# A fused block on one core: expert rows summed in memory by accumulating scatters, and the expert pairs spread over two more units

## What is computed

```python
probs = softmax(x @ Wr); topw, topi = top_k(probs, 4)      # 2048 tokens, 32 experts
shared = silu(x @ Wsg) * (x @ Wsu) @ Wsd                     # 512 -> 1408 -> 512
shared = shared * sigmoid(x @ Wse)
pos = position of each (token, k) in its expert's queue      # kept where pos < 64
ye = (silu(xe @ Wg) * (xe @ Wu)) @ Wd                        # per expert: 64 slots, 512 -> 352 -> 512
out = shared.at[tok].add(ye[sel, posc] * (w * valid))        # up to 4 rows of ye for each token
return x + gb * out
```

## Time and profile before

| | us |
|---|---|
| median of 3 runs | 750.3 (747.75 to 751.67) |
| the profiled run | 753.79 |
| its span, first to last instruction | 751.6 |
| TensorE busy in it | 685.0 |
| VectorE busy | 401.0 |
| ScalarE busy | 296.5 |
| GpSimd busy | 223.0 |

### The profile page before, as it was taken

How to read it: one execution, slowest core, us unless ns; L and a number is a source line. 1 busy time by engine, 2 the same in 40 slices (tenths; PEclk the granted TensorE clock), 3 DMA queues, 4 the chain that set the end, 5 groups by cost and what they waited for, 6 DMA issues and landing times.

```text
span 751.6 us, 9183 instructions
## 1 busy us (share of the span) xinstructions
PE 685.0 (91%) x3297; PEld 476.0 (63%) x3297; DVE 401.0 (53%) x735; ACT 296.5 (39%) x565; POOL 223.0 (30%) x217
## 2 busy tenths in 40 slices
PE   4798888999998799999999999999998999998894
PEld 3565656777666567886665655565564566686673
DVE  3758759678588857762224222122122133688897
ACT  3434785665746623323225333133232143323311
POOL 1254464745436200001000001001000002788883
PEclk9789998999999999999999999999999999999998
DMA  8750000000131004007777877767988772666664
GB/s 270 258 197 0 1 15 28 15 29 15 42 134 63 14 1 140 1 1 258 269 284 291 321 277 263 272 248 284 310 303 302 267 267 80 181 173 193 210 189 147
DMA packets 48328, 124.27 MB, mean 165 GB/s; under 512 B 6152, under 2 KB 10268, under 8 KB 48284
## 3 DMA queue, kind: packets, MB, share of 16 engines
q1 hardware_dynamic: 41884, 102.72, 38.4%
q0 software_dynamic: 6400, 20.98, 9.9%
HBM read 110.83 MB, written 12.85 MB: 165 GB/s over the span
## 4 chain that ended last, share of the span: by engine, by line
PE 37%; DVE 10%; DMA 9%; issue 7%; ACT 3%; POOL 2%; SPq 1%; DVEq 0%; POOLq 0%; ACTq 0%
PE bank L1663 14%; PE bank L1718 9%; PE bank L1675 7%; PE bank L1735 5%; DMA expert_rows<-ye 4%; DMA egu<-in_L_ffn_Wu_dram 3%; DVE egu L1361 2%; ACT xsH L851 1%; DVE prod L1207 1%; DMA xg<-h_rows,slot_tok 1%; DVE ed L1361 1%; DVE egu L1362 1%; PE bank L1706 1%; PE bank L1766 1%; ACT prodH L865 1%
## 5 line engine op out<-in xcount | busy, mean ns | idle before, releaser
L1663 PE MATMUL bank<-xsH,wguH 128*128 128x512 f32 x352 | 144.1, 409 | 7.4 <-issue 2.9
L1663 PE MATMUL bank<-xsL,wguH 128*128 128x512 f32 x352 | 138.3, 393 | 0.0
L1663 PE MATMUL bank<-xsH,wguL 128*128 128x512 f32 x352 | 138.0, 392 | 0.0
L668 POOL DMA_INDIRECT xg<-h_rows,slot_tok x16 | 15.4, 962 | 334.6 <-PE bank L1706 242.1
L1718 PE MATMUL bank<-egu,xeT 128*64 128x352 f32 x512 | 82.6, 477 | 8.9 <-DMA egu<-in_L_ffn_Wu_dram 8.8
L1663 PEld LDWEIGHTS bank<-xsH,wguH 128*128 128x128 f32 x352 | 66.7, 189 | 33.7 <-issue 15.1
L1675 PE MATMUL bank<-wdH,prodH 128*128 128x512 f32 x176 | 74.2, 421 | 12.1 <-DVE prodL L1209 9.6
L865 ACT ACTIVATE prodH<-prod 128x512 fp32r<-128x512 f32 x38 | 24.0, 631 | 140.3 <-DVE prod L1207 133.9
L1663 PEld LDWEIGHTS bank<-xsL,wguH 128*128 128x128 f32 x352 | 66.4, 189 | 14.7
L1663 PEld LDWEIGHTS bank<-xsH,wguL 128*128 128x128 f32 x352 | 66.6, 189 | 12.9 <-issue 0.7
L1207 DVE TENSOR_TENSOR prod<-bank,silu 128x512 f32<-128x512 f32 x38 | 26.2, 688 | 83.3 <-PE bank L1663 60.2
(11 more groups left out here) (225 smaller groups left out, 1117.5 us busy)
## 6 DMA issues: line engine op xcount, KB each, us to landing
egu<-in_L_ffn_Wg_dram SPq DMA_DIRECT2D x32, 704.0 KB
egu<-in_L_ffn_Wu_dram SPq DMA_DIRECT2D x32, 704.0 KB
ed<-in_L_ffn_Wd_dram SPq DMA_DIRECT2D x32, 512.0 KB, 6.1
h2T<-in_L_wmod_dram SPq DMA_DIRECT2D x6, 1024.0 KB, 9.1
ed<-in_L_ffn_Wd_dram SPq DMA_DIRECT2D x32, 192.0 KB, 7.3
expert_rows<-ye SPq DMA_DIRECT2D x17, 256.0 KB, 8.1
h_rows<-ho SPq DMA_DIRECT2D x16, 256.0 KB, 2.0
out_dram<-xres SPq DMA_DIRECT2D x16, 256.0 KB
```

What stands on the lines that cost most here:

```text
L1663: ins = mm.matmul(bk[:, :], l[f][:, w, c, :], r[:, c, :], start=(k == 0), stop=(k == 3 * C - 1))
```

## The change

Five things are changed together.

1. **Sums in memory.** `expert_rows` and the gathers from it are gone. A new array `expert_sums` has one row for each token. SP sets it to zero with 16 stores of 256 KB from the zeroed `ye`, before the first pair's weights. For each pair POOL adds the rows of `ye` to it with two scatters that accumulate in memory (one for each expert of the pair, 64 rows; the second runs over 128 rows, the first 64 of them out of bounds and so skipped). POOL waits for the first before it issues the second, since both experts may have the same token. ACT writes the next pair's rows into `ye` only when both have landed (`added`). SP no longer waits in its loop for anything that has to do with `ye`.
2. **Places.** The 49 stages are spread over the 73 places up to the end of unit 13. The pieces of the last shared weights are asked for two pairs earlier.
3. **The last part.** SP reads all sums back with five plain transfers after the last scatter. DVE joins a tile with one addition. All 16 joins and all 16 gates are on DVE, in units 14 and 15 (`JOINS`, `GATES`). In unit 15 DVE takes the four down results straight from PSUM (`scalar_tensor_tensor`), without ACT's copy.
4. **The table.** `slot_table` makes the destination table `slot_to` as well, and POOL waits for it before the first gather. `y_idx` and its four operations in `slots` are gone.
5. **Order.** `first_rows` of two tiles moves ahead of the low part of tile 1, with POOL's `first_rstd(4)`; `experts_mask` and `pairs_before` move behind the next unit's inputs; PE's `positions` moves behind the second half.

```diff
-        PLACES = [(u, k) for u in range(PAIRS_FROM[0], MERGE) for k in range(2 * PARTS[UNITS[u][0]] + GT)
+        PLACES = [(u, k) for u in range(PAIRS_FROM[0], MERGE + 2) for k in range(2 * PARTS[UNITS[u][0]] + GT)
...
+        JOINS = {(2, 2): (0, 1, 2, 3), (2, 3): (4, 5), (3, 0): (6, 7, 8), (3, 1): (9, 10, 11, 12), (3, 2): (13, 14, 15)}
+        GATES = {(2, 3): (0, 1, 2, 3), (3, 1): (4, 5), (3, 2): (6, 7, 8, 9)}
+        JOINED_FIRST = 12
...
-                    if NP // 2 + 1 <= j < NP // 2 + 4:
+                    if NP // 2 - 1 <= j < NP // 2 + 2:
...
-                    sp.wait_ge(ye_ok, j + 1)
-                    sp.dma_start(ye_dram[j * P:(j + 1) * P, :], ye[:, :]).then_inc(ye_sent, 16)
-                    sp.wait_ge(ye_sent, 16 * (j + 1))
-                    sp.sem_inc(ye_free, 1)
...
+                sp.wait_ge(added, 32 * NP)
+                for k, (i, n) in enumerate(((0, 4), (4, 4), (8, 4), (12, 3), (15, 1))):
+                    at = sums_dram[i * P:(i + n) * P, :].rearrange("(i p) h -> p i h", p=P)
...
+                def add_rows(j):
+                    pool.wait_ge(ye_ok, j + 1)
+                    for e in range(2):
+                        if j or e:
+                            pool.wait_ge(added, 16 * (2 * j + e))
+                        n = (e + 1) * CAP
+                        gp.indirect_dma_start(sums_dram[:, :], bass.IndirectOffsetOnAxis(slot_to[0:n, e, j:j + 1], axis=0),
+                                              ye[0:n, :], None, bounds_check=B * T - 1, oob_is_err=False,
+                                              compute_op=ALU.add).then_inc(added, 16)
...
                 def pair_out(j):
                     act.wait_ge(ey_full, j + 1)
-                    act.wait_ge(ye_free, j + 1)
...
+                        act.wait_ge(added, 32 * j)
...
+                    if n >= LAST_TAKEN:
+                        dve.wait_ge(d_full[m % 2], n // 2 + 1)
+                        dve.wait_ge(y_read, i + 1)
+                        v.scalar_tensor_tensor(xres[:, i, :], dB[m % 2][:, :], sigma[:, i:i + 1], xres[:, i, :],
+                                               ALU.mult, ALU.add).then_inc(d_used[m % 2], 1)
+                        return
...
+                def join(i):
+                    dve.wait_ge(y_in[i // GT if i < NT - 1 else NG], 16)
+                    p = len(PARTS) - (2 if i >= JOINED_FIRST else 1)
+                    dve.wait_ge(x_acc, tile(p, 0, i) - FIRST_TAKEN + 1)
+                    v.tensor_tensor(xres[:, i, :], xres[:, i, :], sum_at[i], ALU.add).then_inc(y_read, 1)
```

More of the change, by code:

```diff
@@ L223, in build @@
         onehot = scr[:, 512:512 + NT * TOP_K * E].rearrange("p (i k e) -> p i k e", k=TOP_K, e=E)
-        top_e, odd, pos, over, idx_f = (scr[:, at:at + NT * TOP_K].rearrange("p (i k) -> p i k", k=TOP_K)
-                                        for at in range(5120, 5120 + 5 * NT * TOP_K, NT * TOP_K))
+        top_e, odd, pos, over = (scr[:, at:at + NT * TOP_K].rearrange("p (i k) -> p i k", k=TOP_K)
+                                 for at in range(5120, 5120 + 4 * NT * TOP_K, NT * TOP_K))
         picked = scd[:, 0:NT * TOP_K * E].rearrange("p (i k e) -> p i k e", k=TOP_K, e=E)
@@ L241, in build @@
         tokB = bank[3][:, 0:3 * NP]
-        YW = TOP_K * H
-        yg = [w.rearrange("p (k h) -> p k h", k=TOP_K) for w in (scr[:, 0:YW], scr[:, YW:2 * YW], scd[:, 0:YW])]
-        NY = len(yg)
+        sum_at = ([scr[:, k * H:(k + 1) * H] for k in range(8)] + [scd[:, k * H:(k + 1) * H] for k in range(4)]
+                  + [scr[:, k * H:(k + 1) * H] for k in range(8, 11)] + [scd[:, 4 * H:5 * H]])
         MERGE = NG * (len(PARTS) - 1)
@@ L523, in _ @@
                 sp.wait_ge(zero_ok, 1)
-                sp.dma_start(ye_dram[E * CAP:E * CAP + P, :], ye[:, :]).then_inc(zero_sent, 16)
+                for i in range(NT):
+                    sp.dma_start(sums_dram[i * P:(i + 1) * P, :], ye[:, :]).then_inc(zero_sent, 16)
                 sp.wait_ge(hot_used, 2 * NG)
@@ L663, in _, with fetch_rows @@
                 gp.memset(ye[:, :], 0.0).then_inc(zero_ok, 1)
-                pool.wait_ge(tab_ok, 1)
-                for j in range(NP):
+                pool.wait_ge(tab_ok, 2)
+                def add_rows(j):
[7 more added lines that the diff above has]
+                                              compute_op=ALU.add).then_inc(added, 16)
+                def fetch_rows(j):
                     if j:
@@ L1103, in _ @@
                 first_var(4)
+                first_rows(HB + 2)
+                first_rows(HB + 3)
                 h_lo(1)
@@ L1401, in _ @@
                         first_var(5)
-                        for i in (HB + 2, HB + 3, 2, 3):
+                        for i in (2, 3):
                             first_rows(i)
@@ L1458, in _ @@
                             experts_ones()
-                        if u == EARLY and f == 1:
-                            experts_mask()
                         if f == 0 and g == 0 and p:
@@ L1501, in _ @@
                         lo_group(*UNITS[u + 1], chunks=range(C // 2, C))
-                    if u >= MERGE and not join_first(g, 2):
-                        combine(g, 2)
-                    if u >= MERGE and join_first(g, 3):
-                        for m in range(3):
-                            last_gate(g * GT + m)
-                        combine(g, 3)
+                    if u == EARLY:
+                        experts_mask()
+                        pairs_before()
+                    if not ahead:
+                        for m in range(10, NT - 1):
+                            last_gate(m)
                     down(p, g, 3)
@@ L1830, in _ @@
                         pair_stages(u, 2 * f)
-                        if u == ROUTE and f == 0:
-                            positions()
                         if u == ROUTE + 2 and f == 0:
@@ L1839, in _ @@
                         half(p, g, f, 1)
+                        if u == ROUTE and f == 0:
+                            positions()
                         pair_stages(u, 2 * f + 1)
```

136 lines of the change are left out of this document (59 added, 77 removed).

## The result

| | us |
|---|---|
| changed kernel, median of 4 runs | 726.4 (724.26 to 729.17) |
| kernel before on the same chip, median of 4 | 750.0 (747.75 to 751.67) |
| ratio | 0.969, 95% interval 0.965 to 0.973 |
| the profiled run of the changed kernel | 729.17, span 727.4 |

What follows compares the result with a forecast made beforehand. TensorE was taken as the bound, busy 685.0 of 751.6 us. The terms sum to -28.4, taking the profiled run from 753.8 to 725.4; with the median 3.5 lower, the forecast was 722 us, range 716 to 740.

Steps and rivals of the forecast that it cites:

- A: First rows of step 1: making two `xhat` rows earlier removes TensorE's idle time and a clock loss, -4.4 us.
- B: Unit 3 to unit 4: mask and scan moved behind the next inputs remove TensorE's idle time and clock loss, -3.7 us.
- C: First gather: the larger table makes POOL start later with nothing to hide it, +1.1 us, up to +2.8.
- D: Expert pairs: SP asks for weights without waiting for the `ye` store, removing TensorE's weight waits and slow clock, -11.5 us.
- E: Last part, unit 12 to the end: two units without joins, then joins and gates in units 14 and 15, -9.9 us.
- The scatters' cycle: Per pair, writing `ye` and two scatters of 7.1 us take 14.9 us, under the shortest period of 16.4: no cost.
- rival 1: Slower scatters set the pairs' pace, cycle 2 s + 0.9 for landing time s; 772 us at s = 11.2; chance 0.10.
- ScalarE never waiting: Sign in the changed profile, against scatters setting the pace: ScalarE never waits for `expert_sums` to land.
- a late scatter stops TensorE within about 2 us: Pairs: ScalarE's waits for scatters hold up `silu`, `prodH` and row copies behind them, so TensorE soon stops.
- the rival's 10 us: Scatters pacing the pairs: only short periods, 738 to 746 us, chance 0.09, or all, 772 us, chance 0.10.
- Rival 3: Gains of A and B are caught by the next engine, VectorE cancels E's; 740 us, 748 with bad D; chance 0.07.

Runs made afterwards that it cites:

- places_12: The changed kernel with the pairs' stages spread only to the end of unit 11, as in the kernel before; 737.2 us, ratio 0.982.
- before_no_wait: The kernel before, but SyncE no longer waits for the store of `ye` to land before asking for the next weights; 740.0 us, ratio 0.989.
- three_scatters: The changed kernel with a third accumulating 64-row scatter per pair, between the two, into an array nothing reads; one time of 742.2 us.

## Why the prediction was right, and where its sum was off

| term | forecast | ledger, first profiles | ledger, second profiles | timed, by the ratios |
|---|---|---|---|---|
| A | -4.4 | -0.9 | -2.9 | -3.7 |
| B | -3.7 | -2.7 | -4.0 | -3.4 |
| C | +1.1 | +2.4 | +0.2 | +3.0 |
| D | -11.5 | -13.2 | -9.6 | -8.3 |
| E | -9.9 | -9.8 | -10.6 | - |
| sum | -28.4 | -24.2 | -26.9 | |

Units 12 and 13 stand between D and E. Without pairs a unit takes 24.9 us (the first silus of units 12, 13 and 14 in places_12 are at 630.67, 655.54 and 680.45), where 24.7 was forecast. D in the ledger is first gate-up to silu, less two such units (304.4 + 14.96 - 49.8 = 269.6 in the first profile of the changed kernel against 282.75 before); E is those two units plus the last stretch (49.8 + 57.2 against 116.9). places_12, whose pairs end with unit 11, shows E by itself: 737.7 - 630.67 = 107.0, so -9.8 and -10.0 against the two profiles of before. The timed values come from undoing the step, each with 2 to 3 us either way; D's is SyncE's wait alone. Their sum with an E of -9.9 is -22.3, and -23.3 was measured by the ratio (-23.6 by the medians); with those intervals the sum alone would prove little.

**A and B** passed as argued: no `xhat` wait, the first half of unit 4 right behind unit 3, and 0.8 us in `positions` where 0.9 was forecast. In the first profile of the changed kernel they fall short, by 3.5 and 1.0 us, where the clock dips of that run lie; that run was 2.8 us above its median.

**D, mechanism right, the term mis-sized.** All its signs came: no weight wait, a mean period of 20.0, the stretch to unit 14 at 320.8 us where 320 was forecast. The after side was right. The before side was one run with 8.8 us of waits where the next had 6.9. The step that failed is the one from the profiled run to the median: "The median of the runs was 750.3, 3.5 us under the profiled run, so the forecast is 722". By the second profile the excess of that run lay mostly in the stretch that term D removes (270.8 against 267.0: 3.8 of the 4.6 us between the spans), so it was taken off twice, once in D and once with the 3.5. With a D smaller by 3.8 the forecast would have been 722 + 3.8 = 725.8; 726.4 was measured. This rests on two profiles and on the 8.3 us of before_no_wait; C, at +3.0 by the ratios, may hold a part of the miss.

**The scatters' cycle** was 2 x 7.1 + 0.7 = 14.9 us in the forecast (15.1 by the formula of rival 1, which has 0.9) and is 18.0 by the table above, 18.1 to 19.0 in the three periods of that trace that it set. The landing was right; missing were POOL's gather for a later pair, which stands ahead of the first scatter (1.3 us), and what the links take beyond the landing. The longest but one of ScalarE's waits, in the timeline of POOL, ScalarE and TensorE:

```profile
569.62 1.01 POOL L674 DMA_INDIRECT xg<-h_rows,slot_tok  x1 [12.37 <-ACT ye L885]
570.94 1.87 POOL L667 DMA_INDIRECT expert_sums<-ye,slot_to  x1 [0.30 <-issue]
578.21 1.99 POOL L667 DMA_INDIRECT expert_sums<-ye,slot_to  x1 [5.40 <-DMA expert_sums<-ye,slot_to]
...
586.80 0.69 ACT L885 ACTIVATE ye<-bank,slot_w 128x512 f32<-128x512 f32 x1 [3.73 <-DMA expert_sums<-ye,slot_to]
587.38 0.59 ACT L864 ACTIVATE xeT<-bank 128x512 f32<-128x512 f32 x1
...
591.26 1.11 PE L1727 MATMUL bank<-egu,xeT 128*64 128x352 f32 x6
```

The cycle is longer than the shortest period that was forecast, 16.4. So "ScalarE never waiting" was wrong, and "a late scatter stops TensorE within about 2 us" as well. Here ScalarE stands 3.7 us, of which 1.7 are past the end of the down product (585.09), and `xeT` is still ready 3 us before the gate-up of 591.26: the half between the two covers it. Two errors cancelled, a chain too short and a cover too thin; that the scatters cost nothing came by this luck. places_12 is where they no longer do, and there the rival's 10 us appear.

**E** came to the pace of its own steps: the wait of 3.2 us (3.3 forecast), unit 14's start to the end in 59.9 and 59.4 us (60.3 forecast). Rival 3 is out.

## What to carry over

A profile's waits are a sample. If the profiled run lies above the median, find the stretch that holds the excess before you subtract it; if the change removes that very stretch, it is already in the term. Second profiles of both kernels, compared by marks in the program, cost one run each and resolved tenths of a microsecond where medians of four runs left two or three. And when a chain is checked against a period, list everything that its engines run in program order between its links, and ask how long the last engine has cover before the bound one starves.

## What was not expected of the hardware

An accumulating scatter of 64 rows holds POOL for 1.6 us (1558 ns in the median), where the gather of 128 rows holds it for 1.0. It lands 3.6 us after its issue at least, and 6.9 in the median beside the weights' traffic. In three_scatters the same scatters took 5.5; that the thinner traffic of the weights is the cause was not isolated. And the granted clock of one stretch of the same program was 0.79 in one run and 1.00 in the next, worth 1.5 us there and, with the longer wait and the dip that followed at 124 us, 3.2 at the first mark. In the runs without this dip the clock had fallen earlier, at 36 to 40 us; nothing in these runs says what decides it.
